# Layer 0 of a graph stack: ScalarE writes the row of beta times the second weight into PSUM, and the second product accumulates onto it

## Chip, core and metric

The kernel runs on one core of a Trainium2 chip. The metric is device time in microseconds of one execution, the median of three runs. The engines of the core work side by side, each through its own queue in order, and wait for each other through semaphores: TensorE (PE in the profile; its weight loads PEld), VectorE (DVE), ScalarE (ACT), GpSimd (POOL) and SyncE (SP), which starts most transfers.

## The reference, cut to what matters

There are 128 graphs of 64 nodes with 512 features, and four layers. Layer 0, the one that the change touches, is a pair of hypergraph convolutions with a layer norm between them:

```python
def hypergraph_conv(x, adj, W, b):
    H = (adj != 0).astype(x.dtype)
    w = adj.reshape(N, -1)[:, :C]
    xw = jnp.einsum('ncd,hd->nch', x, W)
    Dn = 1.0 / einsum('nce,ne->nc', H, w)          # 0 where the sum is 0
    Be = 1.0 / H.sum(axis=1)
    m = Be[:, :, None] * jnp.einsum('nce,nch->neh', H, xw)
    return Dn[:, :, None] * jnp.einsum('nce,neh->nch', H, m) + b
...
h = relu(layernorm(x))
h = relu(hypergraph_conv(h, adj, W1, b1))          # 512 -> 1024
h = layer_norm(h, gamma, beta)                     # beta is a row of 1024
y = hypergraph_conv(h, adj, W2, b2)                # 1024 -> 512
x = x + y + h0                                     # h0: the layer's normed input
```

Layers 1 to 3 (three graph convolutions, a diffusion with attention weights, a mean over neighbours) are computed by other code that the change leaves alone.

## The kernel before

**Tiles and groups.** Two graphs of 64 nodes make a tile of 128 rows, with a block-diagonal 128x128 adjacency. 64 tiles are worked in 16 groups of four; the four tiles of a group are the slots 0 to 3. Each slot has its own two PSUM banks, `ps[:, t, 0]` and `ps[:, t, 1]`, and its own row of every SBUF buffer. The layers run one after the other over all groups. A group's body is unrolled; groups 1 to 14 of a layer are a loop, and the last group has an order of its own, made from the same table.

**Precision.** Each fp32 product is done as three fp32r products of high and low halves (L461 to L463): a producer rounds a value to its high half (`copy`, L690, on ScalarE), and the difference is the low half (`lo_of`, L934 on VectorE, L1265 on GpSimd).

**The steps of a tile in layer 0.** `hyp`: TensorE makes the 128x128 matrix H B H^T from `inc_t` and `binc_hi`, `binc_lo` (L509, L510); ScalarE copies it to `adj_hi` with a sum of its rows (L754), VectorE makes `adj_lo` and sums the degree (L989). `adj0`: the mix of the normed input, transposed (L477, L479). `lin1`: the first weight, 96 products; VectorE applies degree and bias (L1022), ScalarE the relu (L687). `mid`: statistics of 1024 columns on VectorE (L1028, L1031), their root on GpSimd; `midnorm`: ScalarE (L772). `tra`, `trb`: TensorE transposes the two halves (L501), ScalarE and VectorE split them. `lina`, `linb`: the second weight in two halves of 12 matmuls each, both accumulating in `ps[:, t, 1]`, `lina` starting the sum. `linb` is then split to `row_hi`, `row_lo`. `adjb`: the matrix times that row, in `ps[:, t, 0]`; VectorE multiplies by the degree and adds the residual in `x_res` (L1044), which raises the semaphore `final`.

**gamma and beta.** Gamma is multiplied into the second weight at the start. Beta times the second weight is one row, made once by TensorE at the start and kept as `beta_bc` in all partitions. Since beta goes through H B H^T as well, its part of the output is that row times a number per node, the row sum of the matrix times the degree. ScalarE's copy of the matrix yields the row sum (M_SUM), VectorE multiplies (DM_SUM, L1006), and the step `residb` adds the product to the residual (L1036).

**Work for the next group.** Names with `_n` belong to the next group: `stats_n`, `norm_n`, `split_n` (its normed input, split by ScalarE L690 and GpSimd L1265), `hprep_n` and `binc_n` (VectorE: the incidence matrix `inc_t`, and `inc_t` times the reciprocal of the sizes into `binc_w` and `binc_lo`, L983 and L984), `hyp_n`, `adj0_n`, `adj0hi_n`, `deg_n`.

**What sets the order.** `order_hyper()` is a list of (step, slot). Every engine walks the same list and does its part of each step, so the list fixes the order on every engine at once. Before the matrix of the next group's tile can be written into bank 0 of a slot, VectorE must have read the slot's `adjb` result there: `hyp_n` of slot t waits for `final` of slot t (L508).

Of the kernel before, what the change touches and what calls it, by code (L numbers as in the profile page):

```python
# [25 lines left out]
P = 128  # L26
SLOTS = 4
# [10 lines left out]

def order_hyper():
    return [  # L40
        ("resid", 0), ("resid", 1), ("lin1", 0), ("mid", 0), ("lin1", 1), ("hprep_n", 0), ("mid", 1), ("midnorm", 0),
        ("adj0", 3), ("stats_n", 0), ("adj0hi", 3), ("stats_n", 1), ("midnorm", 1), ("lin1", 2), ("residb", 0),
        ("hprep_n", 1), ("mid", 2), ("resid", 2), ("tra", 0), ("hprep_n", 2), ("norm_n", 0), ("tra", 1), ("resid", 3),
        ("midnorm", 2), ("lin1", 3), ("trb", 0), ("lina", 0), ("residb", 1), ("lina", 1), ("mid", 3), ("residb", 2),
        ("tra", 2), ("trb", 1), ("hprep_n", 3), ("linb", 0), ("midnorm", 3), ("norm_n", 1), ("binc_n", 0), ("trb", 2),
        ("stats_n", 2), ("residb", 3), ("lina", 2), ("binc_n", 1), ("tra", 3), ("stats_n", 3), ("adjb", 0),
        ("binc_n", 2), ("split_n", 0), ("linb", 1), ("linb", 2), ("lina", 3), ("trb", 3), ("adjb", 1), ("norm_n", 2),
        ("hyp_n", 0), ("split_n", 1), ("split_n", 2), ("norm_n", 3), ("adjb", 2), ("binc_n", 3), ("linb", 3),
        ("hyp_n", 1), ("hyp_n", 2), ("adj0_n", 0), ("adj0_n", 1), ("adj0hi_n", 0), ("adjb", 3), ("adj0_n", 2),
        ("hyp_n", 3), ("adj0hi_n", 1), ("split_n", 3), ("deg_n", 0), ("adj0hi_n", 2),  # L50
    ]


# [86 lines left out]
def graph_stack(nc, x, adj, adj_t, w0a, w0b, gamma_c, b0a, beta_c, b0b, w1, b1, wv_t, bv_c, aw_c, ab, wk, bk, w3_t, out):  # L140
# [5 lines left out]
    KB = F // P  # L146
    assert 2 * N == P and HID == 2 * F and F == 512 and TILES % SLOTS == 0

    with ExitStack() as ctx:
# [57 lines left out]
        size = sb("size", [P, 4, SLOTS])  # L207
        w_sum = sb("w_sum", [P, SLOTS])
        size_r = sb("size_r", [P, 2, SLOTS], F32R)
        deg = sb("deg", [P, 8, SLOTS])  # L210
        D_SUM, D_POS, D_ZERO, D_SAFE, D_INV, D_OUT, M_SUM, DM_SUM = range(8)
        score = sb("score", [P, 6, SLOTS])
        S_J, S_I, S_IB, S_SUM, S_EPS, S_INV = range(6)
        ps = ctx.enter_context(nc.psum_tensor("ps", [P, SLOTS, 2, F], F32))
# [41 lines left out]
        def f32(ap):  # L256
# [8 lines left out]
        s = sems("", "adj_loaded rows_loaded stats moments deviation norm resid split_hi split_lo "  # L265
                     "final raw_hi raw_lo raw_lo_v raw_scaled cols_loaded vec_loaded b1_loaded wv_loaded "
                     "pool_const ready spread spread_used vec_const vec_out aw_sum const_cols const_sum bk_loaded bk_sum")
        s0 = sems("l0_", "inc w_sum w_hi w_lo size binc hyp m_hi d_sum degree dm_sum "
                         "adj0 adj0_hi adj0_left adj0_lo lin1 affine relu2 stats2 moments2 deviation2 "
                         "norm2 tra tra_hi tra_lo lina trb trb_hi trb_lo linb rowb_hi rowb_lo adjb "  # L270
                         "res_b res_beta")
        s1 = sems("l1_", "asplit_hi asplit_lo " + " ".join(
            f"adj{c} adj{c}_hi adj{c}_left adj{c}_lo lin{c} bias{c} row{c}_hi row{c}_lo" for c in range(3)))
        s2 = sems("l2_", "s_j s_i s_ib diag tr tr_hi tr_lo lin2 row2_hi row2_lo sj score leak exp alpha "
# [184 lines left out]
        def _(pe):  # L459
# [2 lines left out]
                nc.tensor.matmul(out_ap, lhs_hi, rhs_lo, start=False, stop=False, **checks)  # L462
                return nc.tensor.matmul(out_ap, lhs_lo, rhs_hi, start=False, stop=stop, **checks)  # L463

            def linear(bank, t, place, start=True, stop=True):

                for k in range(KB):
                    last = product(ps[:, t, bank, :], col_hi[:, t, k * P:(k + 1) * P], col_lo[:, t, k * P:(k + 1) * P],
                                   w_hi[:, place, k, :], w_lo[:, place, k, :],
                                   start=start and k == 0, stop=stop and k == KB - 1)  # L470
                return last

            def mix_transposed(t):
# [30 lines left out]
            def hyper(g, name, t, i):  # L504
                if name == "hyp":
                    pe.wait_ge(s0["binc"], i)
                    if not first(g):
                        pe.wait_ge(s["final"], i - SLOTS)  # L508
                    nc.tensor.matmul(ps[:, t, 0, 0:P + 2], inc_t[:, t, :], binc_w[:, t, :], start=True, stop=False)  # L509
                    nc.tensor.matmul(ps[:, t, 0, 0:P], inc_t[:, t, :], binc_lo[:, t, :], start=False, stop=True  # L510
                                     ).then_inc(s0["hyp"], 1)
                if name == "adj0":
                    pe.wait_ge(s0["d_sum"], i)
                    pe.wait_ge(s["split_lo"], nl(0, g, t))
                    if first(g) and t == SLOTS - 1:
# [12 lines left out]
                if name == "lina":
                    pe.wait_ge(s0["tra_lo"], i)
                    if first(g):  # L530
                        wait_split(pe, block_end[0])
                    linear(1, t, PLACE[0][2], stop=False).then_inc(s0["lina"], 1)
                if name == "linb":
                    pe.wait_ge(s0["trb_lo"], i)
                    linear(1, t, PLACE[0][3], start=False).then_inc(s0["linb"], 1)
                if name == "adjb":
                    pe.wait_ge(s0["rowb_lo"], i)
                    mix(0, t).then_inc(s0["adjb"], 1)
# [146 lines left out]
        def _(act):  # L685
# [244 lines left out]
        def _(dve):  # L930
# [22 lines left out]
            def hyper(g, name, t, i):  # L953
# [36 lines left out]
                if name == "deg":  # L990
# [11 lines left out]
                    dve.wait_ge(s0["degree"], 5 * g + 4)  # L1002
                    V.tensor_tensor(deg[:, D_OUT, :], deg[:, D_INV, :], deg[:, D_POS, :], ALU.mult
                                    ).then_inc(s0["degree"], 1)
                    dve.wait_ge(s0["degree"], 5 * g + 5)
                    V.tensor_tensor(deg[:, DM_SUM, :], deg[:, D_OUT, :], deg[:, M_SUM, :], ALU.mult  # L1006
                                    ).then_inc(s0["dm_sum"], 1)
                if name == "adj0hi":
                    dve.wait_ge(s0["adj0_hi"], i)
                    if not first(g):  # L1010
# [14 lines left out]
                if name == "mid":  # L1025
# [3 lines left out]
                    dve.wait_ge(s0["stats2"], 2 * i)  # L1029
                    carry_wait()  # L1030
                    V.bn_aggr(moments2[:, t, :], stats2[:, t, :]).then_inc(s0["moments2"], 1)  # L1031
                if name == "residb":

                    dve.wait_ge(s0["res_b"], i)
                    dve.wait_ge(s0["dm_sum"], g + 1)
                    V.scalar_tensor_tensor(x_res[:, t, :], beta_bc[:], deg[:, DM_SUM, t:t + 1], x_res[:, t, :],  # L1036
                                           ALU.mult, ALU.add).then_inc(s0["res_beta"], 1)
                if name == "linb":
                    dve.wait_ge(s0["rowb_hi"], i)
                    lo_of(row_lo[:, t, :], ps[:, t, 1, :], row_hi[:, t, :]).then_inc(s0["rowb_lo"], 1)  # L1040
# [432 lines left out]
```

## Time and profile before

| | |
|---|---|
| median of 3 runs | 2703.79 us (2703.66 to 2704.78) |
| profiled execution, its own time | 2703.96 us |
| its span, first to last instruction | 2702.2 us |
| busy PE / DVE / ACT / POOL | 2660.5 / 2005.8 / 1140.1 / 1162.3 us |
| granted TensorE clock | 0.997 |
| a group of layer 0 in the loop | some 55.8 us, 14 of them |
| last group of layer 0 | 55.56 us |

A busy time is the sum of an engine's instructions. The matmuls overlap: one of 512 columns is shown with 0.39 us, and the next starts 0.23 us after it. So for TensorE the distance from start to start tells more than the busy share: where it is longer than usual, the engine waited. Layer 0 is the time up to 933.55 us.

### The profile page before, as it was taken

How to read it: one execution, taken by the hardware profiler on the slowest of the kernel's cores; microseconds unless marked ns; L12 is line 12 of the kernel's file. 1: busy time of each engine (PE TensorE's matmuls, PEld its weight loads, DVE VectorE, ACT ScalarE, POOL GpSimd, SP SyncE). 2: the span in 40 equal slices, each digit the busy share in tenths (PEclk: the TensorE clock that was granted, in tenths of full speed). 3: DMA queues.
4: the chain of work that ended last, by engine and by line, in shares of the span. 5: the costliest groups of instructions: out<-in, count | busy, mean ns of one | idle time of the engine just before them, and what ended most of it. 6: DMA issues, size and time to landing. Idle time of an engine off the chain costs nothing.

```text
span 2702.2 us, 44745 instructions
## 1 busy us (share of the span) xinstructions
PE 2660.5 (98%) x13218; PEld 2220.7 (82%) x13218; DVE 2005.8 (74%) x4632; ACT 1140.1 (42%) x2103; POOL 1162.3 (43%) x2022
## 2 busy tenths in 40 slices
PE   7999999999999999999999998999999999999999
PEld 5888888888888888888888887888888888888887
DVE  6777777777777776777777778787777777677776
ACT  4444444434444543434343443222223232566665
POOL 5444444444443633434333446212112122677776
PEclk9999999999999999999999999999999999999999
DMA  4111110110111311111111122111111112344443
GB/s 137 38 41 47 37 41 33 45 47 33 41 37 41 106 42 58 44 55 45 54 49 52 47 84 89 57 54 54 52 55 49 54 54 64 114 148 151 134 140 123
DMA packets 136299, 178.58 MB, mean 66 GB/s; under 512 B 54464, under 2 KB 54464, under 8 KB 136256
## 3 DMA queue, kind: packets, MB, share of 16 engines
q1 hardware_dynamic: 131072, 168.62, 19.1%
q10 hardware_dynamic: 5184, 9.44, 1.2%
q8 instruction: 20, 0.33, 0.1%
q14 instruction: 23, 0.19, 0.0%
HBM read 110.90 MB, written 67.11 MB: 66 GB/s over the span
## 4 chain that ended last, share of the span: by engine, by line
PE 94%; DVE 2%; issue 1%; POOL 1%; ACT 1%; DMA 1%; SPq 0%; POOLq 0%; ACTq 0%; DVEq 0%
PE ps L461 27%; PE ps L463 27%; PE ps L462 26%; PE ps L477 6%; PE ps L501 4%; PE ps L479 2%; POOL w_lo L1265 1%; ACT row_hi L690 0%; DVE row_lo L934 0%; PE ps L672 0%; PE ps L576 0%; PE ps L572 0%; DMA raw<-w0a 0%; DMA raw<-w0b 0%; PE ps L509 0%
## 5 line engine op out<-in xcount | busy, mean ns | idle before, releaser
L461 PE MATMUL ps<-w_hi,col_hi 128*128 128x512 f32 x2752 | 1100.5, 400 | 2.0 <-POOL w_lo L1265 0.9
L463 PE MATMUL ps<-w_hi,col_lo 128*128 128x512 f32 x2752 | 1075.5, 391 | 0.0
L462 PE MATMUL ps<-w_lo,col_hi 128*128 128x512 f32 x2752 | 1072.7, 390 | 0.0
L463 PEld LDWEIGHTS ps<-w_hi,col_lo 128*128 128x128 f32 x2752 | 517.1, 188 | 112.6
L461 PEld LDWEIGHTS ps<-w_hi,col_hi 128*128 128x128 f32 x2752 | 517.6, 188 | 106.0 <-issue 4.6
L462 PEld LDWEIGHTS ps<-w_lo,col_hi 128*128 128x128 f32 x2752 | 518.7, 188 | 97.6 <-issue 0.2
L1298 POOL TENSOR_TENSOR var_eps<-moments,eps_ln 128x1 f32<-128x1 f32 x256 | 65.1, 254 | 921.7 <-DVE moments L951 921.4
L690 ACT ACTIVATE col_hi<-ps 128x512 fp32r<-128x512 f32 x448 | 255.4, 577 | 319.3 <-PE ps L479 197.9
L690 ACT ACTIVATE row_hi<-ps 128x512 fp32r<-128x512 f32 x224 | 133.1, 594 | 304.9 <-PE ps L463 303.5
L477 PE MATMUL ps<-adj_both,row_hi 128*128 128x256 f32 x1024 | 252.0, 327 | 5.5 <-DVE deg L989 5.5
L934 DVE TENSOR_TENSOR row_lo<-ps,row_hi 128x512 fp32r<-128x512 f32 x224 | 154.0, 687 | 109.2 <-ACT row_hi L690 107.8
L1265 POOL TENSOR_TENSOR row_lo<-normed,row_hi 128x512 fp32r<-128x512 f32 x128 | 164.6, 1296 | 157.4 <-ACT row_hi L690 156.5
L479 PE MATMUL ps<-adj_both,row_lo 128*128 128x128 f32 x1024 | 227.6, 222 | 0.0
L934 DVE TENSOR_TENSOR col_lo<-ps,col_hi 128x512 fp32r<-128x512 f32 x192 | 121.2, 638 | 133.1 <-ACT col_hi L690 133.1
L730 ACT ACTIVATE normed<-x_in,shift,rstd 128x512 f32<-128x512 f32 x256 | 206.7, 807 | 30.8 <-POOL shift L1304 30.8
L477 PEld LDWEIGHTS ps<-adj_both,row_hi 128*128 128x128 f32 x1024 | 192.8, 188 | 17.0 <-DVE deg L989 7.7
L479 PEld LDWEIGHTS ps<-adj_both,row_lo 128*128 128x128 f32 x1024 | 195.5, 191 | 7.2 <-issue 0.2
L938 DVE TENSOR_TENSOR wide<-ps,col_hi 128x512 f32<-128x512 f32 x256 | 174.9, 683 | 27.5 <-ACT col_hi L690 26.1
L687 ACT ACTIVATE row_hi<-wide 128x512 fp32r<-128x512 f32 x128 | 80.6, 630 | 255.8 <-DVE wide L1059 255.8
L940 DVE TENSOR_TENSOR col_lo<-ps,wide 128x512 fp32r<-128x512 f32 x256 | 177.1, 692 | 8.8
L687 ACT ACTIVATE wide<-wide 128x1024 f32<-128x1024 f32 (+1 forms) x96 | 88.0, 917 | 212.2 <-DVE wide L1022 205.8
L948 DVE BATCH_NORM_STATS2 stats<-x_in 128x6 f32<-128x512 f32 x256 | 174.7, 682 | 0.2
(155 smaller groups left out, 4197.1 us busy)
## 6 DMA issues: line engine op xcount, KB each, us to landing
out<-x_res SPq DMA_DIRECT2D x256, 256.0 KB, 2.0
x_in<-out SPq DMA_DIRECT2D x192, 256.0 KB, 2.7
x_in<-x SPq DMA_DIRECT2D x64, 256.0 KB, 2.6
x_res<-out SPq DMA_DIRECT2D x64, 256.0 KB, 3.2
adj_in<-adj_t SPq DMA_DIRECT2D x96, 64.0 KB, 2.4
raw<-w ACTq DMA_DIRECT2D x12, 256.0 KB, 2.7
raw<-wk ACTq DMA_DIRECT2D x12, 256.0 KB, 2.8
raw<-w_t ACTq DMA_DIRECT2D x10, 256.0 KB, 4.2
```

Of the source, the lines that this page charges most:

```text
L461: nc.tensor.matmul(out_ap, lhs_hi, rhs_hi, start=start, stop=False, **checks)
L462: nc.tensor.matmul(out_ap, lhs_hi, rhs_lo, start=False, stop=False, **checks)
L463: return nc.tensor.matmul(out_ap, lhs_lo, rhs_hi, start=False, stop=stop, **checks)
L477: nc.tensor.matmul(at, row_hi[:, t, k * P:(k + 1) * P], adj_both[:, t, :, :].rearrange("p h n -> p (h n)"), start=True, stop=False)
L479: last = nc.tensor.matmul(at[:, 0:P], row_lo[:, t, k * P:(k + 1) * P], adj_hi[:, t, :], start=False, stop=True)
L690: return nc.scalar.activation(out_ap, in_ap, ACT.Copy)
L730: nc.scalar.activation(normed[:, t, :], x_in[:, t, :], ACT.Relu, bias=shift[:, t:t + 1], scale=rstd[:, t:t + 1]).then_inc(s["norm"], 1)
L934: return V.tensor_tensor(out_ap, full, f32(hi), ALU.subtract)
L938: V.tensor_tensor(blocks(left), halves(t)[0], blocks(f32(col_hi[:, t, :])), ALU.subtract).then_inc(left_done, 1)
L940: return V.tensor_tensor(blocks(col_lo[:, t, :]), halves(t)[1], blocks(left), ALU.add)
L948: V.bn_stats(stats[:, t, 0:6], x_in[:, t, :]).then_inc(s["stats"], 1)
L1265: return Q.tensor_tensor(out_ap, full, f32(hi), ALU.subtract)
```

## The change

Beta's row now enters ahead of the second weight's product instead of behind the last one. After the relu of `lin1`, ScalarE copies `beta_bc` (SBUF) into `ps[:, t, 1, :]`, semaphore `seeded`. `lina` waits for it and no longer starts the sum: its matmuls add onto the row. The row sum in ScalarE's copy of the matrix, VectorE's product DM_SUM and the four `residb` steps a group go. `adjb` on VectorE waits for GpSimd's residual (`res_b`) directly. The affine step of `lin1` waits for the degree. The table of the order is another one.

```diff
-                    linear(1, t, PLACE[0][2], stop=False).then_inc(s0["lina"], 1)
+
+                    pe.wait_ge(s0["seeded"], i)
+                    linear(1, t, PLACE[0][2], start=False, stop=False, skip_group_check=True).then_inc(s0["lina"], 1)
...
-                    if not first(g):
-                        act.wait_ge(s0["dm_sum"], g)
-                    nc.scalar.activation(adj_hi[:, t, :], ps[:, t, 0, 0:P], ACT.Copy,
-                                         accum_out=deg[:, M_SUM, t:t + 1]).then_inc(s0["m_hi"], 1)
+                    copy(adj_hi[:, t, :], ps[:, t, 0, 0:P]).then_inc(s0["m_hi"], 1)
...
                     relu(wide[:, t, :], wide[:, t, :]).then_inc(s0["relu2"], 1)
+                    if first(g):
+                        act.wait_ge(s["vec_out"], 2)
+                    copy(ps[:, t, 1, :], beta_bc[:]).then_inc(s0["seeded"], 1)
...
-                    dve.wait_ge(s0["degree"], 5 * g + 5)
-                    V.tensor_tensor(deg[:, DM_SUM, :], deg[:, D_OUT, :], deg[:, M_SUM, :], ALU.mult
-                                    ).then_inc(s0["dm_sum"], 1)
...
                     dve.wait_ge(s0["lin1"], i)
+                    dve.wait_ge(s0["degree"], 5 * g + 5)
...
-                if name == "residb":
-
-                    dve.wait_ge(s0["res_b"], i)
-                    dve.wait_ge(s0["dm_sum"], g + 1)
-                    V.scalar_tensor_tensor(x_res[:, t, :], beta_bc[:], deg[:, DM_SUM, t:t + 1], x_res[:, t, :],
-                                           ALU.mult, ALU.add).then_inc(s0["res_beta"], 1)
...
                     dve.wait_ge(s0["adjb"], i)
-                    dve.wait_ge(s0["res_beta"], i)
+                    dve.wait_ge(s0["res_b"], i)
...
-        ("hyp_n", 0), ("split_n", 1), ("split_n", 2), ("norm_n", 3), ("adjb", 2), ("binc_n", 3), ("linb", 3),
+        ("split_n", 1), ("split_n", 2), ("norm_n", 3), ("binc_n", 3), ("adjb", 2), ("linb", 3), ("hyp_n", 1),
```

On TensorE the new table moves one step: `linb` of slot 1 stood behind `tra` of slot 3 and `adjb` of slot 0, and now stands ahead of them. On VectorE and GpSimd more is moved. Two places of the loop's body are shown.

VectorE, late in a group, before. The first row splits the transposed half of slot 3 (`trb`), then come `adjb` of slot 1, `hyp_n` of slot 0 (two rows), `adjb` of slot 2, `binc_n` of slot 3 (two rows) and `linb` of slot 3:

```order
L934 TENSOR_TENSOR col_lo<-ps,col_hi 128x512 [waits l0_trb_hi]
L1044 SCALAR_TENSOR_TENSOR x_res<-ps,deg,x_res 128x512 [waits l0_res_beta,l0_adjb]
L934 TENSOR_TENSOR adj_both<-ps,adj_both 128x128 [waits l0_m_hi]
L989 TENSOR_REDUCE deg<-ps 128x1
L1044 SCALAR_TENSOR_TENSOR x_res<-ps,deg,x_res 128x512 [waits l0_res_beta,l0_adjb]
L983 TENSOR_SCALAR binc_w<-inc_t,size_r 128x128 [waits l0_size]
L984 TENSOR_SCALAR binc_lo<-inc_t,size_r 128x128
L934 TENSOR_TENSOR row_lo<-ps,row_hi 128x512 [waits l0_rowb_hi]
```

The same place in the changed kernel, whose line numbers are other ones:

```order
L936 TENSOR_TENSOR col_lo<-ps,col_hi 128x512 [waits l0_trb_hi]
L1038 SCALAR_TENSOR_TENSOR x_res<-ps,deg,x_res 128x512 [waits l0_res_b,l0_adjb]
L936 TENSOR_TENSOR adj_both<-ps,adj_both 128x128 [waits l0_m_hi]
L991 TENSOR_REDUCE deg<-ps 128x1
L985 TENSOR_SCALAR binc_w<-inc_t,size_r 128x128 [waits l0_size]
L986 TENSOR_SCALAR binc_lo<-inc_t,size_r 128x128
L1038 SCALAR_TENSOR_TENSOR x_res<-ps,deg,x_res 128x512 [waits l0_res_b,l0_adjb]
L936 TENSOR_TENSOR row_lo<-ps,row_hi 128x512 [waits l0_rowb_hi]
```

`binc_n` of slot 3 has moved ahead of `adjb` of slot 2.

ScalarE at the start of a group, before: the relus of `lin1` of slots 0 and 1, `midnorm` 0, the copy of `adj0` of slot 3, `midnorm` 1:

```order
L687 ACTIVATE wide<-wide 128x1024 [waits l0_affine]
L768 REGISTER_ALU
L687 ACTIVATE wide<-wide 128x1024 [waits l0_affine]
L771 REGISTER_ALU
L772 ACTIVATE wide<-wide,shift2,rstd2 128x1024 [waits l0_deviation2]
L757 REGISTER_ALU
L690 ACTIVATE col_hi<-ps 128x512 [waits l0_adj0]
L771 REGISTER_ALU
L772 ACTIVATE wide<-wide,shift2,rstd2 128x1024 [waits l0_deviation2]
```

The same place in the changed kernel:

```order
L689 ACTIVATE wide<-wide 128x1024 [waits l0_affine]
L692 ACTIVATE ps<-beta_bc 128x512
L767 REGISTER_ALU
L689 ACTIVATE wide<-wide 128x1024 [waits l0_affine]
L692 ACTIVATE ps<-beta_bc 128x512
L756 REGISTER_ALU
L692 ACTIVATE col_hi<-ps 128x512 [waits l0_adj0]
L773 REGISTER_ALU
L774 ACTIVATE wide<-wide,shift,rstd 128x1024 [waits l0_deviation2]
L773 REGISTER_ALU
L774 ACTIVATE wide<-wide,shift,rstd 128x1024 [waits l0_deviation2]
```

Each relu has a copy of `beta_bc` into PSUM behind it, and the copy of `adj0` stands ahead of both `midnorm` steps.

## Rows read from the trace of the kernel before

**Rows 1.** The page, part 1: busy us, share of the span, instructions.
```profile
PE 2660.5 (98%) x13218; PEld 2220.7 (82%) x13218; DVE 2005.8 (74%) x4632; ACT 1140.1 (42%) x2103; POOL 1162.3 (43%) x2022
```

**Rows 2.** Busy time by stretch: one loop group of layer 0, then its last.
```profile
core 0: us, PE busy (x) PEld busy (x) DVE busy (x) ACT busy (x) POOL busy (x), PEclk, DMA share, GB/s
375.88:431.65 55.77, 55.27 (x276) 46.22 (x277) 42.10 (x97) 24.02 (x42) 24.31 (x44) 1.00 0.13 40
877.99:933.55 55.56, 54.69 (x270) 45.00 (x270) 37.71 (x68) 29.62 (x49) 40.83 (x59) 1.00 0.35 107
```

**Rows 3.** Waits of PE from 96 to 878 us: us in total, times, longest.
```profile
PE ps L477 <- DVE deg L989: 5.1, 14, 0.4
```

**Rows 4.** Timeline of PE: start us, us, what, idle before and releaser.
```profile
426.68 0.27 PE L509 MATMUL ps<-binc_w,inc_t 128*128 128x130 f32 x1
...
427.76 0.22 PE L479 MATMUL ps<-adj_both,row_lo 128*128 128x128 f32 x1
428.35 0.39 PE L477 MATMUL ps<-adj_both,row_hi 128*128 128x256 f32 x1 [0.36 <-DVE deg L989]
...
431.17 0.30 PE L509 MATMUL ps<-binc_w,inc_t 128*128 128x130 f32 x1
```

**Rows 5.** Timeline of DVE in the same stretch.
```profile
424.37 0.15 DVE L989 TENSOR_REDUCE deg<-ps 128x1 f32<-128x2 f32 x1
424.44 0.74 DVE L1044 SCALAR_TENSOR_TENSOR x_res<-ps,deg,x_res 128x512 f32<-128x512 f32 x1
425.09 0.72 DVE L983 TENSOR_SCALAR binc_w<-inc_t,size_r 128x128 fp32r<-128x128 f32 x1
425.73 1.33 DVE L984 TENSOR_SCALAR binc_lo<-inc_t,size_r 128x128 fp32r<-128x128 f32 x1
427.34 0.69 DVE L934 TENSOR_TENSOR row_lo<-ps,row_hi 128x512 fp32r<-128x512 f32 x1 [0.28 <-ACT row_hi L690]
...
428.14 0.15 DVE L989 TENSOR_REDUCE deg<-ps 128x1 f32<-128x2 f32 x1
...
429.38 0.69 DVE L940 TENSOR_TENSOR col_lo<-ps,wide 128x512 fp32r<-128x512 f32 x1
430.27 0.75 DVE L1044 SCALAR_TENSOR_TENSOR x_res<-ps,deg,x_res 128x512 f32<-128x512 f32 x1 [0.20 <-PE ps L463]
```

**Rows 6.** Timeline of ACT in the same stretch, and of POOL.
```profile
423.48 0.27 ACT L754 ACTIVATE adj_both<-ps 128x128 fp32r<-128x128 f32 x1
423.63 0.20 ACT L754 ACTIVATION_READ_ACCUMULATOR adj_both<-ps 128x1 f32 x1
423.73 1.15 ACT L690 ACTIVATE row_hi<-normed 128x512 fp32r<-128x512 f32 x2
...
424.43 2.55 POOL L1265 TENSOR_TENSOR row_lo<-normed,row_hi 128x512 fp32r<-128x512 f32 x2 [4.83 <-ACT row_hi L690]
```

**Rows 7.** L984 alone (duration ns min/median/max); timeline of DVE and POOL in layer 2.
```profile
L984 DVE TENSOR_SCALAR binc_lo<-inc_t,size_r x64: 278/281/1327, 12.2 to 872.3; 128x128 fp32r<-128x128 f32 x64
...
1644.72 1.31 DVE L1089 TENSOR_SCALAR inc_t<-ident,score 128x128 fp32r<-128x128 f32 x1
...
1644.66 1.29 POOL L1265 TENSOR_TENSOR w_lo<-raw,w_hi 128x512 fp32r<-128x512 f32 x1 [4.40 <-ACT w_hi L690]
```

**Rows 8.** Groups by shape, 96 to 934 us: busy us, mean ns | idle before.
```profile
L1036 DVE SCALAR_TENSOR_TENSOR x_res<-beta_bc,deg,x_res 128x512 f32<-128x512 f32 x60 | 46.3, 772 | 0.0
L690 ACT ACTIVATE row_hi<-normed 128x512 fp32r<-128x512 f32 x60 | 36.3, 630 | 0.7
L754 ACT ACTIVATION_READ_ACCUMULATOR adj_both<-ps 128x1 f32 x57 | 11.7, 206 | 0.0
```

**Rows 9.** Timeline of ACT at the start of a group, around `midnorm`.
```profile
446.39 0.58 ACT L690 ACTIVATE col_hi<-ps 128x512 fp32r<-128x512 f32 x1
448.15 1.24 ACT L772 ACTIVATE wide<-wide,shift,rstd 128x1024 f32<-128x1024 f32 x1 [1.18 <-POOL shift L1329]
```

**Rows 10.** Timeline of PE in the last group of layer 0: `trb` 2 and `tra` 3.
```profile
911.37 0.39 PE L463 MATMUL ps<-w_hi,col_lo 128*128 128x512 f32 x1
912.03 0.66 PE L501 MATMUL ps<-ident,wide 128*128 128x128 f32 x4 [0.27 <-DVE col_lo L934]
...
915.06 0.39 PE L463 MATMUL ps<-w_hi,col_lo 128*128 128x512 f32 x1
915.91 0.66 PE L501 MATMUL ps<-ident,wide 128*128 128x128 f32 x4 [0.46 <-ACT wide L772]
```

More of the change, by code:

```diff
@@ L40, in order_hyper @@
     return [
[L41 to L47, printed above, removed]
-        ("hyp_n", 0), ("split_n", 1), ("split_n", 2), ("norm_n", 3), ("adjb", 2), ("binc_n", 3), ("linb", 3),
-        ("hyp_n", 1), ("hyp_n", 2), ("adj0_n", 0), ("adj0_n", 1), ("adj0hi_n", 0), ("adjb", 3), ("adj0_n", 2),
-        ("hyp_n", 3), ("adj0hi_n", 1), ("split_n", 3), ("deg_n", 0), ("adj0hi_n", 2),
+        ("resid", 0), ("resid", 1), ("lin1", 0), ("mid", 0), ("lin1", 1), ("hprep_n", 0), ("adj0", 3), ("mid", 1),
+        ("stats_n", 0), ("adj0hi", 3), ("midnorm", 0), ("midnorm", 1), ("resid", 2), ("lin1", 2), ("hprep_n", 1),
+        ("mid", 2), ("stats_n", 1), ("tra", 0), ("hprep_n", 2), ("norm_n", 0), ("tra", 1), ("resid", 3),
+        ("midnorm", 2), ("lin1", 3), ("trb", 0), ("lina", 0), ("lina", 1), ("mid", 3), ("tra", 2), ("trb", 1),
+        ("hprep_n", 3), ("linb", 0), ("midnorm", 3), ("norm_n", 1), ("trb", 2), ("stats_n", 2), ("lina", 2),
+        ("binc_n", 0), ("binc_n", 1), ("linb", 1), ("tra", 3), ("stats_n", 3), ("adjb", 0), ("binc_n", 2),
+        ("split_n", 0), ("linb", 2), ("lina", 3), ("trb", 3), ("adjb", 1), ("norm_n", 2), ("hyp_n", 0),
+        ("split_n", 1), ("split_n", 2), ("norm_n", 3), ("binc_n", 3), ("adjb", 2), ("linb", 3), ("hyp_n", 1),
+        ("hyp_n", 2), ("adj0_n", 0), ("adj0_n", 1), ("adj0hi_n", 0), ("adjb", 3), ("adj0hi_n", 1), ("adj0_n", 2),
+        ("hyp_n", 3), ("split_n", 3), ("adj0hi_n", 2), ("deg_n", 0),
     ]
@@ L209, in graph_stack @@
         size_r = sb("size_r", [P, 2, SLOTS], F32R)
-        deg = sb("deg", [P, 8, SLOTS])
-        D_SUM, D_POS, D_ZERO, D_SAFE, D_INV, D_OUT, M_SUM, DM_SUM = range(8)
+        deg = sb("deg", [P, 6, SLOTS])
+        D_SUM, D_POS, D_ZERO, D_SAFE, D_INV, D_OUT = range(6)
         score = sb("score", [P, 6, SLOTS])
@@ L267, in graph_stack @@
                      "pool_const ready spread spread_used vec_const vec_out aw_sum const_cols const_sum bk_loaded bk_sum")
-        s0 = sems("l0_", "inc w_sum w_hi w_lo size binc hyp m_hi d_sum degree dm_sum "
+        s0 = sems("l0_", "inc w_sum w_hi w_lo size binc hyp m_hi d_sum degree "
                          "adj0 adj0_hi adj0_left adj0_lo lin1 affine relu2 stats2 moments2 deviation2 "
                          "norm2 tra tra_hi tra_lo lina trb trb_hi trb_lo linb rowb_hi rowb_lo adjb "
-                         "res_b res_beta")
+                         "res_b seeded")
         s1 = sems("l1_", "asplit_hi asplit_lo " + " ".join(
@@ L463, in product, with linear @@
                 return nc.tensor.matmul(out_ap, lhs_lo, rhs_hi, start=False, stop=stop, **checks)
-            def linear(bank, t, place, start=True, stop=True):
+            def linear(bank, t, place, start=True, stop=True, **checks):
                 for k in range(KB):
@@ L469, in linear @@
                                    w_hi[:, place, k, :], w_lo[:, place, k, :],
-                                   start=start and k == 0, stop=stop and k == KB - 1)
+                                   start=start and k == 0, stop=stop and k == KB - 1, **checks)
                 return last
@@ L531, in hyper @@
                         wait_split(pe, block_end[0])
-                    linear(1, t, PLACE[0][2], stop=False).then_inc(s0["lina"], 1)
+                    pe.wait_ge(s0["seeded"], i)
+                    linear(1, t, PLACE[0][2], start=False, stop=False, skip_group_check=True).then_inc(s0["lina"], 1)
                 if name == "linb":
                     pe.wait_ge(s0["trb_lo"], i)
-                    linear(1, t, PLACE[0][3], start=False).then_inc(s0["linb"], 1)
+                    linear(1, t, PLACE[0][3], start=False, skip_group_check=True).then_inc(s0["linb"], 1)
                 if name == "adjb":
```

## The prediction

> **What bounds the kernel.** I read the page's busy times first: TensorE is busy for 98% of the span, VectorE for 74%, the others for under half [rows 1]. A busy TensorE can still be late, so next I cut layer 0 into its groups. A loop group takes 55.77 us, of which TensorE is busy for 55.27 [rows 2]; the fourteen loop groups lie between 55.6 and 56.1. Time can be won or lost only where the distance between two matmuls is not the usual one. The list of TensorE's waits over the loop has one line, 14 times 0.4 us at most [rows 3]: the first matmul of `adj0_n` of slot 1, which waits for VectorE's degree sum. The timeline shows its size: the matmul ahead of it started at 427.76, and where nothing waits a successor follows such a one after 0.06, so 427.82; it started at 428.35, 0.53 late [rows 4]. All else of the loop is TensorE at its pace, with a granted clock of 1.00 [rows 2]. So busy time that goes from VectorE (four additions of 0.77 us a group [rows 8]) or comes onto ScalarE counts for nothing by itself. What counts is what each engine has to finish just before a matmul that is close behind it.
>
> **What the change does, part by part.**
>
> The seeds: 64 copies of 128x512 on ScalarE. No row shows ScalarE writing PSUM from SBUF. The nearest is the copy from SBUF to SBUF, 0.63 us [rows 8]; I take that, with 0.3 (half) and 1.2 (twice) as bounds. It adds 40 us to an engine that is busy 24.0 us of 55.77 in a group [rows 2]. The tightest place is the second `midnorm`, for whose result TensorE's transposes wait with hardly any room: ahead of it ScalarE stood idle for 1.18 us, waiting for GpSimd [rows 9]. One seed lands in that stretch (that of slot 1), and 0.63 fits into 1.18. `seeded` itself comes some 10 us before `lina` wants it. Cost: 0. Above 1.18 it would cost its excess in each group.
>
> What goes: 206 ns of accumulator reading in each of ScalarE's matrix copies, VectorE's 64 additions and 16 small products. They ran beside TensorE's work, and none of them released it. Gain by themselves: 0. The waits added (`seeded` on TensorE, the degree on VectorE's affine step) are for things done earlier; the affine step stands behind the degree in VectorE's own order anyway. Cost: 0.
>
> `linb` of slot 1 moved up on TensorE: the same matmuls in another order, no cost in the loop. In the last group, though, TensorE waits twice there. `trb` 2 started 0.66 after the matmul ahead instead of the usual 0.23, and `tra` 3 0.85 after instead of 0.23 [rows 10]. The first waited for VectorE, which had two of the removed additions ahead; the second waited for ScalarE's `midnorm`, and now has 2.7 us (12 matmuls) more ahead of it. Both should go: 0.43 + 0.62 = 1.05 us, once. The bounds are 0 and 1.3.
>
> **The move that I think decides: `binc_n` of slot 3 ahead of `adjb` of slot 2.** `binc_n` is two small VectorE operations, usually 0.28 us each. Before the change, at this place, they took 0.72 and 1.33 [rows 5]; the second form ranges from 278 to 1327 ns [rows 7]. Beside them GpSimd ran two `row_lo` operations, 2.55 us together from 424.43, so about 424.43 to 425.71 and on to 426.98 [rows 6]. The first VectorE operation ended at 425.81 and the second at 427.06, each 0.1 after an end of GpSimd's. I read this as: such an operation of VectorE waits until the GpSimd operation under way is over. Before, that was harmless, since VectorE was early for `linb`'s result anyway (idle 0.28 [rows 5]). Now `adjb` of slot 2 stands behind it, and TensorE's `hyp_n` of slot 2 waits for `final` of that.
>
> Step by step, in the times of rows 4 to 6:
> - ScalarE loses the accumulator read at 423.63, so its `row_hi` copies start there instead of 423.73, and GpSimd at 424.33 [rows 6].
> - VectorE's reduction starts at 424.37 and its next operation at 424.44 [rows 5]. That is now `binc_w`, 0.11 after GpSimd's start. It ends with GpSimd's first operation, at 425.7, and `binc_lo` with the second, at 426.96.
> - `adjb` of slot 2 starts just before that end, as neighbours do (425.73 against 425.81), at 426.88, and takes 0.74: 427.62. From a VectorE end to a matmul it is 0.06 (428.14 + 0.15 to 428.35). `hyp_n` of slot 2 starts at 427.68 instead of 426.68: **+1.00**.
> - The first matmul of `adj0_n` 1 comes 1.14 behind it (426.68 to 427.82), at 428.82. Its own wait is over by then: `row_lo` starts at 427.54 instead of 427.34, and the degree sum ends at 428.49. Against 428.35: **+0.47**. The old 0.53 is absorbed.
> - `hyp_n` of slot 3 waits for `final` of slot 3. VectorE's `adj0hi_n` 0 hangs on `adj0_n` 0, which is 1.0 later, so its second operation starts at 430.38 instead of 429.38. `adjb` 3 follows some 0.61 later, at 430.99 instead of 430.27, and ends at 431.74; TensorE goes on at 431.80 instead of 431.17 [rows 4, 5]: **+0.62** a group.
>
> Fifteen groups (0 to 14) hold a `binc_n`: 15 x 0.62 = 9.3 us. The bounds are 15 x 0.47 = 7.1, if VectorE catches up at slot 3, and 15 x 1.00 = 15.0, if nothing is absorbed. **Sum:** 2703.96 (the profiled execution's own time) + 9.3 - 1.05 = 2712.2. That execution lies 0.17 above the median of the runs, so I say 2712.0.
>
> By the Trainium skill, "SBUF — State Buffer", section "Who interferes with whom", the pair of ports that VectorE and GpSimd share is taken whole by the instruction that issues first, and the other "fully blocks". If the engines shared bandwidth instead, `binc_w` and `binc_lo` would need perhaps twice their 0.28, be done at 425.4, and the change would cost nothing at this place. The trace agrees with the page (1.33 beside GpSimd, 0.28 alone).
>
> **The rivals.**
>
> *VectorE gets in first: no change.* If `binc_w` starts ahead of GpSimd, it runs its 0.28, and only `binc_lo` waits for one GpSimd operation, until 425.7. `adjb` 2 then ends at 426.4, before TensorE wants it at 426.68. That leaves 2703.8 - 1.05 = 2702.7. The margin that decides is the 0.11 us above. For my side: in layer 2 a VectorE operation that started 0.06 after GpSimd's waited its 1.31 us out [rows 7], and `binc_lo` waited though it was issued just about when GpSimd's second operation began. Against me: the 0.10 that ScalarE saves is an inference, and without it the margin is 0.01.
>
> *Faster.* If the accumulator read was what held the degree sum back, or the lighter VectorE reaches it sooner, the 0.53 goes from every group: 15 x 0.53 = 8.0, with the 1.05, 2694.8. Against it: the operation ahead of the matrix split, `row_lo` at 427.34, waited for the other copy, `row_hi` [rows 5], and that chain is not shortened.
>
> *ScalarE too late: slower by more.* If a seed costs over 1.18 us, `midnorm` 1 is late. At 1.5 us, 0.3 x 15 = 5 on top: 2717.
>
> **How the numbers follow.** Three runs of before lie within 0.04%, and 0.2% (5.4 us) is about what a measurement of this kernel tells from no change. The blocked `binc_n` (forecast) 0.70, VectorE first 0.20, faster 0.04, ScalarE too late 0.06. Slower by over 0.2% is forecast and last rival, 0.76; within it the second and a little of the forecast's low end, nothing else; I give 0.20 and 0.04 to the others. The likeliest case's own range is 2709.5 to 2716, from 7.1 to 12 a layer less the 0 to 1.3. To leave out no more than 2 in 10 the range must take in the case of no change: 2702.0 to 2716.
>
> **What the changed profile would show.** L985 at some 1.26 us and L986 at 1.33 once in each group; `final` of slot 2 as what releases `hyp_n` 2 on TensorE, some 1 us idle; the wait for the degree sum gone; loop groups of 56.4 us; the seeds at 0.6 us with no matmul waiting for `seeded`; no waits at `trb` 2 and `tra` 3 in the last group. I am wrong if L985 takes 0.28 there, or if GpSimd's `row_lo` starts behind it.

## The result, and the profile after

The changed kernel takes 2713.84 us (median of 7 runs, 2713.2 to 2715.83), the kernel before 2704.72 us beside it (7 runs, 2703.66 to 2705.82). The ratio is 1.0036, its 95% interval 1.0026 to 1.0046: slower by 9.1 us. The profiled execution is that of 2713.84 us, with a span of 2711.9 (before: 2702.2).

The page's busy times (us, share of the span, instructions), to be held against [rows 1]:

```profile
PE 2658.2 (98%) x13218; PEld 2219.8 (82%) x13218; DVE 1966.0 (72%) x4552; ACT 1168.7 (43%) x2103; POOL 1150.0 (42%) x2022
```

Each engine's load moved as the diff says: VectorE has 40 us less, ScalarE 29 more, TensorE is as busy as it was. None of that shows where 9 us went. The span has to be cut into stretches. First the busy time of a loop group of layer 0 and of its last group, as in [rows 2]:

```profile
core 0: us, PE busy (x) PEld busy (x) DVE busy (x) ACT busy (x) POOL busy (x), PEclk, DMA share, GB/s
378.50:435.03 56.53, 55.28 (x278) 46.24 (x277) 39.74 (x93) 25.91 (x40) 23.57 (x44) 1.00 0.13 39
888.80:943.49 54.69, 54.25 (x270) 45.15 (x270) 32.88 (x63) 31.29 (x52) 39.62 (x59) 1.00 0.37 109
```

In the loop group TensorE is busy for the same 55.28 us as before (55.27), but the group lasts 56.53 in place of 55.77 (most of its fellows took 55.8). The last group is shorter, 54.69 in place of 55.56. Layer 1 takes 706.0 us in both traces. So the loss is waiting time in layer 0, in the groups that prepare a next one. TensorE's waits from 96 to 878 us (us in total, times, longest), where [rows 3] had one line of 5.1 us:

```profile
PE ps L509 <- DVE x_res L1038: 15.6, 27, 0.8
```

The old wait for the degree sum is gone, and another stands in its place, three times as large: `hyp_n` waits for `adjb`, VectorE's line 1038. It comes twice a group. The timeline of TensorE, around what [rows 4] showed:

```profile
430.95 0.27 PE L510 MATMUL ps<-binc_lo,inc_t 128*128 128x128 f32 x1
432.05 0.33 PE L509 MATMUL ps<-binc_w,inc_t 128*128 128x130 f32 x1 [0.83 <-DVE x_res L1038]
...
433.25 0.33 PE L477 MATMUL ps<-adj_both,row_hi 128*128 128x256 f32 x1
...
436.30 0.30 PE L509 MATMUL ps<-binc_w,inc_t 128*128 128x130 f32 x1 [0.34 <-DVE x_res L1038]
```

`hyp_n` of slot 2 stood idle for 0.83 and of slot 3 for 0.34. Between them `adj0_n` of slot 1 (433.25) starts with no wait at all. VectorE in the same stretch, for [rows 5]:

```profile
428.55 0.28 DVE L936 TENSOR_TENSOR adj_both<-ps,adj_both 128x128 fp32r<-128x128 f32 x1
428.75 0.15 DVE L991 TENSOR_REDUCE deg<-ps 128x1 f32<-128x2 f32 x1
428.82 1.28 DVE L985 TENSOR_SCALAR binc_w<-inc_t,size_r 128x128 fp32r<-128x128 f32 x1
430.02 1.32 DVE L986 TENSOR_SCALAR binc_lo<-inc_t,size_r 128x128 fp32r<-128x128 f32 x1
431.26 0.74 DVE L1038 SCALAR_TENSOR_TENSOR x_res<-ps,deg,x_res 128x512 f32<-128x512 f32 x1
431.92 0.67 DVE L936 TENSOR_TENSOR row_lo<-ps,row_hi 128x512 fp32r<-128x512 f32 x1
...
434.80 0.69 DVE L942 TENSOR_TENSOR col_lo<-ps,wide 128x512 fp32r<-128x512 f32 x1
435.41 0.74 DVE L1038 SCALAR_TENSOR_TENSOR x_res<-ps,deg,x_res 128x512 f32<-128x512 f32 x1
```

And GpSimd there, for [rows 6]:

```profile
428.72 2.53 POOL L1259 TENSOR_TENSOR row_lo<-normed,row_hi 128x512 fp32r<-128x512 f32 x2 [3.94 <-ACT row_hi L692]
```

This is the suspected cause in one picture; the experiments test it. GpSimd starts two `row_lo` at 428.72. VectorE's `binc_w` starts 0.10 later, and it takes 1.28 where 0.28 is usual; `binc_lo` takes 1.32. `adjb` 2 can begin only at 431.26, ends at 432.00, and TensorE goes on at 432.05. In the old order `adjb` 2 stood ahead of these two and was not touched by what befell them.

### The profile page after: what moved, and what is told of

It reads as the page before. It is cut to its first block, busy times and chain, and to the rows that moved or that the text cites. A ratio compares the mean times of both kernels' runs of the same rounds, so it can differ in the third digit from the quotient of the medians.

```text
span 2711.9 us, 44619 instructions
## 1 busy us (share of the span) xinstructions
PE 2658.2 (98%) x13218; PEld 2219.8 (82%) x13218; DVE 1966.0 (72%) x4552; ACT 1168.7 (43%) x2103; POOL 1150.0 (42%) x2022
## 4 chain that ended last, share of the span: by engine, by line
PE 90%; DVE 4%; issue 2%; ACT 1%; POOL 1%; DMA 0%; SPq 0%; POOLq 0%; ACTq 0%; DVEq 0%
PE ps L461 26%; PE ps L463 26%; PE ps L462 26%; PE ps L477 5%; PE ps L501 4%; PE ps L479 2%; DVE x_res L1038 1%; DVE binc_lo L986 1%; ACT col_hi L692 1%; DVE binc_w L985 1%; DVE wide L940 0%; POOL w_lo L1259 0%; PE ps L509 0%; ACT w_hi L692 0%; PE ps L578 0%
```

## The experiments

The times of the experiments are medians of 5 to 11 runs, beside 15 to 27 of the kernel before on the same chip. "Lead" is how long before `binc_w` of slot 3 GpSimd's `row_lo` of slot 1 started, from the timelines; the group is a middle one of the loop.

| kernel | time, us | before, us | ratio, 95% interval | lead, us | `binc_w`, us | group, us |
|---|---|---|---|---|---|---|
| before | | | | 0.66 | 0.72 | 55.8 |
| changed | 2713.84 | 2704.72 | 1.0036 [1.0026, 1.0046] | 0.10 | 1.28 | 56.5 |
| 1 `adjb` 2 back ahead | 2704.08 | 2704.41 | 0.9998 [0.9989, 1.0007] | 0.76 | 0.62 | 55.8 |
| 2 `binc_n` 3 earlier still | 2704.21 | 2704.41 | 1.0000 [0.9990, 1.0009] | none near | 0.28 | 55.8 |
| 3 the swap alone, old kernel | 2716.32 | 2704.41 | 1.0048 [1.0034, 1.0061] | 0.01 | 1.37 | 56.6 |
| 4 the seeds alone, old table | 2704.57 | 2704.41 | 1.0000 [0.9991, 1.0009] | 0.76 | 0.62 | 55.8 |
| 5 GpSimd held back | 2704.27 | 2704.66 | 0.9997 [0.9988, 1.0006] | -0.04 | 0.28 | 55.8 |
| 6 another TensorE order | 2700.74 | 2704.66 | 0.9986 [0.9977, 0.9995] | none near | 0.28 | 55.5 |
| 7 two seeds | 2704.75 | 2704.60 | 1.0001 [0.9992, 1.0010] | 0.76 | 0.62 | 55.8 |
| 8 four seeds | 2724.96 | 2704.66 | 1.0075 [1.0061, 1.0089] | 0.76 | 0.62 | 56.9 |

### 1. Only the swap undone

```diff
-        ("split_n", 1), ("split_n", 2), ("norm_n", 3), ("binc_n", 3), ("adjb", 2), ("linb", 3), ("hyp_n", 1),
+        ("split_n", 1), ("split_n", 2), ("norm_n", 3), ("adjb", 2), ("binc_n", 3), ("linb", 3), ("hyp_n", 1),
```

> The changed kernel with adjb 2 put back ahead of binc_n 3 in the order of TensorE's operations; the seeds from ScalarE and the rest of the change stay. Theory (GpSimd's row_lo goes ahead of VectorE's two operations at L985 and L986 because binc_n 3 comes first, so adjb 2's product comes 0.7 us late in each group): the group's period falls from 56.5 to about 55.8 us, L985 and L986 no longer take 1.28 and 1.33 us once a group, and the time is 2702.5 to 2704.5 us. Rival (the seeds on ScalarE, or the rest of the table's change, cost the 9 us): it stays at 2713 us.

2704.08 us: the whole loss is gone with one pair of entries turned round. The seeds, the removed additions and the rest of the new table cost nothing measurable together. One part of the expectation was wrong in its detail: `binc_w` and `binc_lo` are not short again. They still wait for GpSimd, only with `adjb` 2 already done. VectorE in this kernel, the same place:

```profile
424.74 0.74 DVE L1038 SCALAR_TENSOR_TENSOR x_res<-ps,deg,x_res 128x512 f32<-128x512 f32 x1
425.39 0.62 DVE L985 TENSOR_SCALAR binc_w<-inc_t,size_r 128x128 fp32r<-128x128 f32 x1
425.94 1.32 DVE L986 TENSOR_SCALAR binc_lo<-inc_t,size_r 128x128 fp32r<-128x128 f32 x1
```

GpSimd's pair:

```profile
424.63 2.54 POOL L1259 TENSOR_TENSOR row_lo<-normed,row_hi 128x512 fp32r<-128x512 f32 x2 [3.94 <-ACT row_hi L692]
```

The same long wait of VectorE does harm in one place and none in the other. TensorE's waits from 96 to 885 us have their old form:

```profile
PE ps L477 <- DVE deg L991: 5.1, 14, 0.4
```

### 2. The order kept, `binc_n` 3 at a quiet time

```diff
-        ("split_n", 0), ("linb", 2), ("lina", 3), ("trb", 3), ("adjb", 1), ("norm_n", 2), ("hyp_n", 0),
-        ("split_n", 1), ("split_n", 2), ("norm_n", 3), ("binc_n", 3), ("adjb", 2), ("linb", 3), ("hyp_n", 1),
+        ("split_n", 0), ("linb", 2), ("binc_n", 3), ("lina", 3), ("trb", 3), ("adjb", 1), ("norm_n", 2), ("hyp_n", 0),
+        ("split_n", 1), ("split_n", 2), ("norm_n", 3), ("adjb", 2), ("linb", 3), ("hyp_n", 1),
```

> The changed kernel with binc_n 3 moved still further ahead, to right behind linb 2, so that it is still ahead of adjb 2 but GpSimd's row_lo is issued at a time at which it is through before VectorE's L985 and L986 begin. Theory (the pair of VectorE and GpSimd decides): L985 and L986 take 0.28 us each in all their calls, and the time is 2702 to 2706 us. Rival (what costs is the product's row of binc_n 3 standing ahead of adjb 2 on TensorE and VectorE, whoever holds the pair): it stays at 2711 to 2714 us.

2704.21 us. `binc_n` 3 is still ahead of `adjb` 2, so the order on VectorE is not by itself what costs. `binc_w` and `binc_lo` run 4 us before GpSimd's two `row_lo`, and take 0.28 each. (GpSimd's `row_lo` of slot 0 still runs for 0.03 us when `binc_w` starts, which shows in neither.) The two `row_lo` now meet other operations of VectorE. GpSimd first:

```profile
423.71 2.54 POOL L1259 TENSOR_TENSOR row_lo<-normed,row_hi 128x512 fp32r<-128x512 f32 x2 [3.95 <-ACT row_hi L692]
```

VectorE in that stretch:

```profile
419.73 0.28 DVE L985 TENSOR_SCALAR binc_w<-inc_t,size_r 128x128 fp32r<-128x128 f32 x1
419.92 0.28 DVE L986 TENSOR_SCALAR binc_lo<-inc_t,size_r 128x128 fp32r<-128x128 f32 x1
...
423.74 0.15 DVE L991 TENSOR_REDUCE deg<-ps 128x1 f32<-128x2 f32 x1
423.81 0.74 DVE L1038 SCALAR_TENSOR_TENSOR x_res<-ps,deg,x_res 128x512 f32<-128x512 f32 x1
```

`adjb` 2 starts 0.10 behind GpSimd, just as `binc_w` did in the changed kernel, and takes its usual 0.74. It has one large input in PSUM and one in SBUF. The two of `binc_n` read nothing but SBUF, one large input each. By the Trainium skill, "GPSIMD Engine Reference", section "Key points", the two engines contend where VectorE is in a mode that uses both ports or has two inputs in SBUF; the trace agrees in that `binc_w` is held (1.28) and `adjb` is not (0.74). With one large input it would have to be the mode that counts for `binc_n`, and no run shows which mode an operation is in.

### 3. The swap alone, on the kernel before

```diff
-        ("hyp_n", 0), ("split_n", 1), ("split_n", 2), ("norm_n", 3), ("adjb", 2), ("binc_n", 3), ("linb", 3),
+        ("hyp_n", 0), ("split_n", 1), ("split_n", 2), ("norm_n", 3), ("binc_n", 3), ("adjb", 2), ("linb", 3),
```

> The kernel before with binc_n 3 put ahead of adjb 2 and nothing else: TensorE still makes the beta row's product. Theory: GpSimd's row_lo stands ahead of VectorE's L983 and L984 in 15 groups, each group is 0.65 to 0.85 us longer, and the time is 2713 to 2717 us, with no gain in the last group. Rival (VectorE goes first here, or the cost came with the seeds): 2704 to 2705 us.

2716.32 us, 11.9 above before, more than the whole change costs. So the loss needs neither the seeds nor anything else of the diff. ScalarE still reads its accumulator here, GpSimd starts later relative to VectorE, and the lead is down to what the records can just resolve. VectorE:

```profile
430.12 0.15 DVE L989 TENSOR_REDUCE deg<-ps 128x1 f32<-128x2 f32 x1
430.18 1.37 DVE L983 TENSOR_SCALAR binc_w<-inc_t,size_r 128x128 fp32r<-128x128 f32 x1
431.48 1.32 DVE L984 TENSOR_SCALAR binc_lo<-inc_t,size_r 128x128 fp32r<-128x128 f32 x1
```

GpSimd:

```profile
430.18 2.54 POOL L1265 TENSOR_TENSOR row_lo<-normed,row_hi 128x512 fp32r<-128x512 f32 x2 [4.83 <-ACT row_hi L690]
```

GpSimd is first by 0.004 to 0.008 us in all 15 groups, and gets its way each time. `binc_w` waits the longer for it, 1.37, and the group is 0.1 us longer than in the changed kernel.

### 4. The seeds alone

The changed kernel's code, with the table of the kernel before less its four `residb` entries (so `linb` 1 and the `midnorm` steps are back in their old places too). The line that matters most:

```diff
-        ("split_n", 1), ("split_n", 2), ("norm_n", 3), ("binc_n", 3), ("adjb", 2), ("linb", 3), ("hyp_n", 1),
+        ("hyp_n", 0), ("split_n", 1), ("split_n", 2), ("norm_n", 3), ("adjb", 2), ("binc_n", 3), ("linb", 3),
...
```

> The changed kernel's seeds from ScalarE with the order table of the kernel before, less its entries for the beta row. Theory (64 seeds of 0.58 us on ScalarE are hidden in its idle time and the products removed had been no part of the path): 2703 to 2705.5 us, no matmul waiting for a seed. Rival (ScalarE's seeds cost the time): 2709 us or more.

2704.57 us against 2704.41. Writing the row on ScalarE in place of 64 additions on VectorE is worth nothing and costs nothing that the times can tell.

### 5. GpSimd held back by 0.2 us

The order of the changed kernel is kept. GpSimd computes a small product into a spare column, whose value nobody reads.

```diff
                 pool.wait_ge(s["split_hi"], nl(layer, g, t))
+                if layer == 0 and not first(g) and t == 1:
+                    for _ in range(1):
+                        Q.tensor_tensor(spare[:, _:_ + 1], eps_ln[:], minus_one, ALU.mult)
                 lo_of(row_lo[:, t, :], normed[:, t, :], row_hi[:, t, :]).then_inc(s["split_lo"], 1)
```

> The changed kernel, its order table kept, with one small operation (128x1, about 0.2 us by the rows of the changed kernel, its result unused) put on GpSimd ahead of its row_lo of slot 1, from the second group on. In the profile of the changed kernel GpSimd's row_lo began 0.10 us ahead of VectorE's binc_w at L985; here it begins about 0.1 us behind it. Theory (the engine that begins first goes first): L985 takes 0.28 us in every call, at most L986 waits, adjb 2's product is ready in time, the loop's groups are back at 55.8 us and the time is 2702.5 to 2705 us. Rival (GpSimd's two operations win over VectorE's short ones in any case, or the order of TensorE's work costs the time by itself): 2712 us or more.

2704.27 us: more work on GpSimd, and some 9.5 us less than the changed kernel. GpSimd:

```profile
425.39 0.19 POOL L1306 TENSOR_TENSOR spare<-eps_ln,consts 128x1 f32<-128x1 f32 x1 [3.95 <-ACT row_hi L693]
425.53 2.64 POOL L1260 TENSOR_TENSOR row_lo<-normed,row_hi 128x512 fp32r<-128x512 f32 x2
```

VectorE:

```profile
425.43 0.15 DVE L992 TENSOR_REDUCE deg<-ps 128x1 f32<-128x2 f32 x1
425.49 0.28 DVE L986 TENSOR_SCALAR binc_w<-inc_t,size_r 128x128 fp32r<-128x128 f32 x1
425.68 1.33 DVE L987 TENSOR_SCALAR binc_lo<-inc_t,size_r 128x128 fp32r<-128x128 f32 x1
426.94 0.74 DVE L1039 SCALAR_TENSOR_TENSOR x_res<-ps,deg,x_res 128x512 f32<-128x512 f32 x1
```

`binc_w` is first by 0.04 (I had expected 0.1) and takes 0.28, in all 15 groups. GpSimd's pair is longer than elsewhere by 0.10 (2.64 against 2.54), all of it in the first of the two (1.40 against 1.30), and it gets in between VectorE's two operations: `binc_lo` waits for one `row_lo`, not for two. From the reduction's start `adjb` 2 begins after 1.51 us, in the changed kernel after 2.51, and no matmul waits for it. This is the prediction's rival "VectorE gets in first", made to happen: which of two cases holds hangs on 0.14 us of GpSimd's start.

### 6. A version meant to beat both

The kernel of experiment 2, with the matmuls that need the degree sum moved back (the lines are shown as experiment 2 breaks them):

```diff
-        ("hyp_n", 2), ("adj0_n", 0), ("adj0_n", 1), ("adj0hi_n", 0), ("adjb", 3), ("adj0hi_n", 1), ("adj0_n", 2),
+        ("hyp_n", 2), ("adj0_n", 0), ("adj0hi_n", 0), ("adjb", 3), ("adj0_n", 1), ("adj0hi_n", 1), ("adj0_n", 2),
```

> A version meant to beat both: the kernel of the second experiment (binc_n 3 right behind linb 2) with adj0hi_n 0 and adjb 3 moved ahead of adj0_n 1, so that the 0.36 us for which TensorE waits once a group for VectorE's reduction ahead of adj0_n 1 is filled. Theory (that wait is on the path and nothing takes its place): 0.25 to 0.36 us a group for 15 groups, less up to 0.6 us in the last group where adjb 3 now waits, so 3 to 5 us: 2699 to 2702 us. Rival (adjb 3 now waits for VectorE's row_lo in each group and gives it back): 2703 to 2706 us.

2700.74 us, 3.9 under before, and 13.1 under the changed kernel's median (on another chip). The interval of the ratio ends at 0.9995, so it is faster, though by less than the 0.2% that the prediction took as its bound. A loop group, which takes 55.8 in experiment 2:

```profile
375.60:431.10 55.50, 55.30 (x277) 46.24 (x276) 37.74 (x93) 25.69 (x40) 23.55 (x45) 1.00 0.13 40
```

The list of TensorE's waits from 96 to 878 us is empty. In the last group, as expected, `adjb` 3 waits:

```profile
PE ps L460 <- DVE row_lo L935: 0.5, 1, 0.5
```

### 7 and 8. How much room ScalarE has

Each seed is written twice or four times, on the kernel of experiment 1:

```diff
+                    for c in range(4):
+                        if c:
+                            act.wait_ge(s0["seeded"], 4 * i - 4 + c)
+                        copy(ps[:, t, 1, :], beta_bc[:]).then_inc(s0["seeded"], 1)
-                    copy(ps[:, t, 1, :], beta_bc[:]).then_inc(s0["seeded"], 1)
...
-                    pe.wait_ge(s0["seeded"], i)
+                    pe.wait_ge(s0["seeded"], 4 * i)
```

> The kernel of the first experiment (adjb 2 back ahead of binc_n 3) with each seed written four times by ScalarE, one after the other, so 1.7 to 2.2 us more per tile on ScalarE; what is computed is the same. By the rival of the prediction (ScalarE too late, once a seed takes more than the 1.18 us that ScalarE was idle ahead of midnorm 1) this costs about 13 us or more: 2717 us and above. Theory that ScalarE has more room than that idle time, since midnorm 1's product is not needed at once: at most 0.15 us a group and a little in the last one, 2704 to 2709 us.

2724.96 us, 20.3 above before. Here my second thought, that ScalarE had more room than its idle time showed, fell, and the prediction's rival held. TensorE's waits from 96 to 878 us:

```profile
PE ps L501 <- ACT wide L777: 9.7, 28, 0.5
PE ps L477 <- DVE deg L994: 4.8, 13, 0.4
```

Two transposes a group wait for `midnorm`. ScalarE is busy without a break there, with the four copies ahead of both:

```profile
396.14 2.49 ACT L692 ACTIVATE ps<-beta_bc 128x512 f32<-128x512 f32 x4
398.56 0.58 ACT L692 ACTIVATE col_hi<-ps 128x512 fp32r<-128x512 f32 x1
399.04 2.37 ACT L777 ACTIVATE wide<-wide,shift,rstd 128x1024 f32<-128x1024 f32 x2
```

With two copies:

> As with four seeds, but each seed written twice: about 1.1 to 1.2 us on ScalarE per tile in place of 0.58, just under the 1.18 us of idle time ahead of midnorm 1 from which the prediction's rival (ScalarE too late) was to decide. By that rival's threshold nothing is late: 2702.5 to 2705.5 us, no matmul waiting for midnorm. If each further seed costs its share of what four cost (20 us for three more), it is about 2711 us.

2704.75 us, no change, and in the loop `midnorm` is not among what TensorE waits for. In the last group of layer 0 it is: one wait of 0.4 us in experiment 1 is 1.0 us here, too little for the times to tell. Two copies hold ScalarE for 1.15 us from the first's start to what follows, four for 2.42 (396.14 to 398.56 above). For the loop the edge lies between them, and the 1.18 us of [rows 9] is in that interval; where exactly was not measured. The price fits as well: 2.42 less 1.18 is 1.24 us a group, and the groups are 1.16 longer than in experiment 1.

## Why the prediction was right

The forecast was 2712.0 us, the range 2702 to 2716, slower with a chance of 0.76. It came out at 2713.84. As a difference, 8.2 us were forecast and 9.1 measured; the other half of the 1.8 us between the times is the kernel before, whose median beside it was 2704.72 in place of the 2703.79 that I started from.

- **What bounds.** Right: TensorE's busy time in a loop group did not move (55.27, 55.28), only its waits did.
- **The seeds cost 0.** Right, as far as the times can tell, by experiments 4 and 7. I took 0.63 us for one; it is 0.582 (median of 64). ScalarE's idle time ahead of `midnorm` 1 fell from 1.18 to 0.65 us, by about one seed:

```profile
450.38 0.58 ACT L692 ACTIVATE ps<-beta_bc 128x512 f32<-128x512 f32 x1
450.89 0.58 ACT L692 ACTIVATE col_hi<-ps 128x512 fp32r<-128x512 f32 x1
451.37 1.23 ACT L774 ACTIVATE wide<-wide,shift,rstd 128x1024 f32<-128x1024 f32 x1
453.26 1.24 ACT L774 ACTIVATE wide<-wide,shift,rstd 128x1024 f32<-128x1024 f32 x1 [0.65 <-POOL shift L1323]
```

- **What goes is worth 0.** Right, by experiment 4.
- **GpSimd first, by 0.11 us.** Right: 0.10 in all 15 groups. The inference behind it, that ScalarE saves the 0.10 of the accumulator read, fits the pairs of runs: with the read the leads are 0.66 and 0.01, without it 0.76 and 0.10. No run took out the read alone. My fear that a lead of 0.01 might not be enough was unfounded (experiment 3).
- **`hyp_n` 2 +1.00, `adj0_n` 1 +0.47, `hyp_n` 3 +0.62.** Counted from the start of `trb` 3, they are +0.99, +0.52 and +0.75. The third is the term that was mis-sized. `adjb` 3 itself came as I had said: `trb` 3 started at 421.64 before and at 426.02 here, 4.38 apart, so 435.41 is 431.03 in the times of the forecast, which was 430.99. But I let TensorE follow its end after 0.06, which is the distance seen behind a reduction. Behind `adjb` 3 the rows of before had 0.15: 430.27 + 0.75 to 431.17 [rows 4, 5]. After the change it is 0.15 again (435.41 + 0.74 to 436.30). So `hyp_n` 3 is 0.13 later than forecast, 0.04 for `adjb` 3 and 0.09 for this distance. The period of the loop groups grew by 0.71, not 0.62 (55.82 to 56.53 between groups 2 and 13); the other 0.04 is made up again before the next group. Up to the last group the loss is 10.8 us against my 9.3: 1.0 of the 1.5 is in the fourteen loop groups (9.7 against 8.7), and 0.5 is in what stands ahead of them, which ends 1.12 later instead of 0.62. That 0.5 is the transfers' timing and not the change's: from 20 to 98 us TensorE waits 4.3 us for the weights `w0b` by DMA, in the kernel before 3.8, and 1.8 to 4.6 over the ten traces. Behind `adjb` 2 0.06 was right (432.00 to 432.05). Why the two differ I did not test.
- **The last group -1.05.** It was -0.87 in the profiles, and the step is only half right. The waits at `trb` 2 and `tra` 3 are gone, but an earlier transpose in the group now waits longer for `midnorm`. TensorE's waits in the changed kernel's last group:

```profile
PE ps L501 <- ACT wide L774: 0.4, 1, 0.4
```

  And what took them away is not settled: in experiment 3, whose last group has the old program, the wait at `tra` 3 is gone too, and the group takes 54.9 us against 55.56. So 0.62 of my 1.05 may have been one execution's timing. The last group of before is longer than those of the changed kernel and of experiments 1 to 5 (54.7 to 55.0), and a term that rests on a single event in it was worth less trust than one that repeats 14 times. It is too small for the times to tell.
- **The rivals.** "VectorE in first" was 0.10 to 0.14 us of start away (experiments 3 and 5). "ScalarE too late" has a threshold and a price that fit (experiments 7 and 8); 1.5 us was not tried. At 2.42 us a tile, 17 of the 20 us stand ahead of the last group, and the rest in it. "Faster" did not happen: in experiment 1 the degree sum is as late as before.

## What to carry over

Putting a short VectorE operation that reads only SBUF ahead of one on which TensorE waits is a risk if GpSimd works on SBUF at that time: it costs not its own 0.28 us but up to one GpSimd operation, 1.3 us here. So compare start times on both engines, to 0.1 us and finer, before moving it, and move it to where GpSimd is idle instead. An operation's long time in a profile that harms nothing (`binc_lo` 1.33 before) is a warning of what it will cost at another place. Busy times moved by 40 us from one engine to another here and were worth nothing; a table entry moved by one place was worth 10 to 12.

## What the runs showed of the hardware

- Who starts first decides, down to the resolution of the trace: with a lead of 0.004 to 0.008 us GpSimd held VectorE off for 1.1 us 15 times of 15 (experiment 3), with 0.04 the other way `binc_w` was never held (experiment 5).
- VectorE's two operations in a row are not one to GpSimd: it gets in between them (experiment 5), and its pair is 0.10 us longer for it. In the changed kernel `binc_w` has its turn at the end of the first `row_lo` without making the pair longer (2.53 us).
- VectorE's degree operations on 128x4 values show the same rule at a small size, beside GpSimd's residual additions, with no experiment at all (duration in ns, min/median/max). In the kernel before:

```profile
L995 DVE TENSOR_SCALAR deg<-deg x16: 170/1212/1218, 30.4 to 880.5; 128x4 f32<-128x4 f32 x16
L998 DVE SCALAR_TENSOR_TENSOR deg<-deg x16: 161/162/165, 30.6 to 881.8; 128x4 f32<-128x4 f32 x16
```

  The same two and a reciprocal in the changed kernel:

```profile
L997 DVE TENSOR_SCALAR deg<-deg x16: 169/170/171, 30.0 to 892.5; 128x4 f32<-128x4 f32 x16
L1000 DVE SCALAR_TENSOR_TENSOR deg<-deg x16: 163/1136/1139, 30.2 to 892.7; 128x4 f32<-128x4 f32 x16
L1003 DVE RECIPROCAL deg<-deg x16: 177/178/180, 30.4 to 893.9; 128x4 f32<-128x4 f32 x16
```

  In the loop, the first is 0.10 behind an addition of GpSimd before the change and 0.02 ahead of one after it; the second is 0.02 ahead before and 0.19 behind after. Behind, each takes 1.1 to 1.2 us, ahead 0.16 to 0.17. The reciprocal starts while GpSimd is at work (0.18 behind its start before, 0.09 after) and takes 0.18 either way: not every operation on SBUF is held.
- ScalarE's copy of 128x512 from SBUF into PSUM is quicker than the same within SBUF:

```profile
L692 ACT ACTIVATE ps<-beta_bc x64: 578/582/585, 49.1 to 915.7; 128x512 f32<-128x512 f32 x64
L692 ACT ACTIVATE row_hi<-normed x128: 616/625/632, 19.4 to 1604.1; 128x512 fp32r<-128x512 f32 x128
```

  A copy from PSUM to SBUF takes 598 ns. A relu from SBUF to SBUF that writes f32 takes 626 on average, so the type written is not what differs. By the Trainium skill, "ScalarE: Activation LUTs", section "Step-by-step: what each stage is for", ScalarE reaches PSUM faster than SBUF with what it writes; the trace agrees, by 43 ns.
